# Weighted expert masks: from eight TensorE turns and two copies a batch to one small turn and a trip through DRAM; one weight split a unit later

## The reference, cut to what matters

```
router_logits = xf @ Wr.T
probs = softmax(router_logits)
topw, topi = top_k(probs, 2)
expert_w = sum(one_hot(topi, 8) * topw[..., None], axis=1)
for each expert e:
    g_lora = xf @ Ag_e.T @ Bg_e.T * 2
    u_lora = xf @ Au_e.T @ Bu_e.T * 2
    h = silu(gate_base + g_lora) * (up_base + u_lora)
    d_delta = h @ Ad_e.T @ Bd_e.T * 2
    acc = acc + d_delta * expert_w[:, e]
```

## Time and profile before

| | |
|---|---|
| median of 3 runs | 714.2 us (712.54 to 715.79) |
| profiled execution, its own time | 712.47 us |
| its span (first to last instruction) | 710.7 us |
| outside the span | 1.77 us |
| PE busy | 688.0 us, 97% |
| DVE busy | 517.6 us, 73% |
| ACT busy | 376.0 us, 53% |
| granted TensorE clock, mean | 0.996 |

### The profile page before, as it was taken

One profiled execution on the slowest core, in us unless ns is written; L12 is line 12 of the kernel. 1 busy time (PEld: TensorE's weight loads), 2 busy tenths in 40 slices (PEclk: granted clock), 3 DMA queues, 4 the chain that ended last, 5 costly groups with the idle time before them and its releaser, 6 DMA issues.

```text
span 710.7 us, 10703 instructions
## 1 busy us (share of the span) xinstructions
PE 688.0 (97%) x4090; PEld 585.9 (82%) x4090; DVE 517.6 (73%) x933; ACT 376.0 (53%) x777; POOL 130.9 (18%) x125
## 2 busy tenths in 40 slices
PE   7999999999999999999999999999999999999997
PEld 7778888878777788887888878887777888889886
DVE  7736667886965658556675656757769998998996
ACT  5896676855745425354254442446557355354541
POOL 7145434510000010000200001000032214203220
PEclk9999999999999999999999999999999999999999
DMA  5096353000000000000000000050000000000000
GB/s 192 13 309 213 106 136 98 0 1 1 1 1 0 1 1 1 0 1 1 1 1 0 1 1 1 0 237 2 1 0 1 1 1 30 1 30 1 2 30 30
DMA packets 21282, 25.78 MB, mean 36 GB/s; under 512 B 976, under 2 KB 19408, under 8 KB 20464
## 3 DMA queue, kind: packets, MB, share of 16 engines
q1 hardware_dynamic: 20576, 23.79, 10.2%
q10 hardware_dynamic: 656, 1.31, 0.5%
HBM read 22.94 MB, written 2.16 MB: 35 GB/s over the span
## 4 chain that ended last, share of the span: by engine, by line
PE 70%; DVE 18%; issue 5%; ACT 4%; POOL 2%; DMA 1%; DVEq 0%; POOLq 0%
PE bank L89 21%; PE bank L91 19%; PE bank L90 19%; DVE l_ring_lo L2472 2%; PE bank L490 2%; DVE l_ge L2453 2%; DVE l_h L2468 2%; DVE l_o L2476 1%; DVE l_h L2425 1%; DVE h_raw L1186 1%; POOL m_den L827 1%; PE bank L466 1%; DVE fused_lo L141 1%; DVE l_oT_lo L2482 1%; POOL l_prod L2336 1%
## 5 line engine op out<-in xcount | busy, mean ns | idle before, releaser
L1186 DVE TENSOR_TENSOR h_raw<-h_s,bank 128x512 f32<-128x512 f32 x104 | 71.4, 687 | 113.8 <-ACT h_s L1176 98.8
L1176 ACT ACTIVATE h_s<-bank 128x512 f32<-128x512 f32 x104 | 62.2, 598 | 161.2 <-PE bank L91 161.1
L1191 DVE TENSOR_TENSOR h_ring_lo<-h_raw,h_ring_hi 128x512 fp32r<-128x512 f32 x92 | 69.0, 750 | 0.1
L1180 ACT ACTIVATE h_ring_hi<-h_raw 128x512 fp32r<-128x512 f32 x104 | 64.8, 623 | 2.3 <-DVE h_raw L1186 2.3
L90 PE MATMUL bank<-fused_lo,h_ring_hi 128*128 128x256 f32 x208 | 58.4, 281 | 0.0
L2173 ACT ACTIVATE l_s<-bank 128x512 f32<-128x512 f32 x32 | 19.1, 598 | 64.6 <-PE bank L91 64.6
L89 PE MATMUL bank<-l_xT_hi,l_wgu 128*128 128x512 f32 x128 | 51.3, 401 | 0.1
L89 PE MATMUL bank<-f_yT_hi,mlp_hi 128*128 128x512 f32 x128 | 50.9, 398 | 0.0
L90 PE MATMUL bank<-l_xT_lo,l_wgu 128*128 128x512 f32 x128 | 50.3, 393 | 0.0
L91 PE MATMUL bank<-l_xT_hi,l_lo 128*128 128x512 f32 x128 | 50.3, 393 | 0.0
L91 PE MATMUL bank<-f_yT_hi,fused_lo 128*128 128x512 f32 x128 | 50.0, 391 | 0.0
(11 more groups left out here) (363 smaller groups left out, 2022.8 us busy)
## 6 DMA issues: line engine op xcount, KB each, us to landing
m_W<-m_scratch SPq DMA_DIRECT2D x16, 512.0 KB, 6.2
fused_raw<-in_fused SPq DMA_DIRECT2D x1, 3584.0 KB, 16.0
res<-in_x SPq DMA_DIRECT2D x4, 512.0 KB, 6.1
fused_raw<-in_fused SPq DMA_DIRECT2D x2, 1024.0 KB, 8.3
l_raw<-in_layer SPq DMA_DIRECT2D x1, 2048.0 KB, 10.0
out_x<-res SPq DMA_DIRECT2D x16, 128.0 KB, 1.8
l_raw<-in_layer SPq DMA_DIRECT2D x1, 1280.0 KB, 12.5
fused_raw<-in_fused SPq DMA_DIRECT2D x1, 1152.0 KB, 5.1
```

Of the source, the lines that this page charges most:

```text
L1176: self.nc.scalar.activation(self.s[u % 2][r, :], gate[r, :], ACT.Silu).then_inc(self.silu.sem, 1)
L1180: self.nc.scalar.activation(self.unit(i, u)[0], self.product(i, u), ACT.Copy).then_inc(self.hi.sem, 1)
L1186: self.nc.vector.tensor_tensor(out=self.product(i, u), in0=self.s[u % 2][r, :], in1=up[r, :], op=ALU.mult).then_inc(self.hidden.sem, 1)
L1191: self.nc.vector.tensor_tensor(out=lo, in0=self.product(i, u), in1=f32(hi), op=ALU.subtract).then_inc(self.lo.sem, 1)
```

## The change

Four things are changed.

1. The weighted masks are no longer widened by DVE and turned by PE in eight 128x128 transposes. DVE writes both weighted tiles, [128, 32] each, side by side with the columns in the order (expert, chunk), and PE turns the 64 columns in one instruction (`turn_weights`, position 9). ACT copies the result, 64 rows x 128 tokens, to SBUF (`turned_sel`, in memory that `selx[2]` had).
2. SP stores these 64 rows to a DRAM tensor `expert_weights` (32 KB) and then loads each of the two [8, 512] halves back with every row repeated 16 times, into `mask[:, n, :]`: two DMAs of 256 KB.
3. The waits follow: `weigh_experts` waits for the two loads (`weights_spread`); `scale_y` of the next batch, whose output lies over `turned_sel`, waits for the store; the squeeze waits for the copy (t = 1) and for `operands(1)` (t = 2).
4. In the first batch the piece `squeeze` is split at position 10, not 9, by ACT and by DVE.

```diff
+        g.expert_weights = nc.dram_tensor("expert_weights", (B, 2, E, S), fp32, kind="Internal").ap()
...
-    SPLIT = {..., 8: ("down",), 9: ("squeeze",), 11: ("base2",), 12: ("back",)}
+    SPLIT = {..., 8: ("down",), 10: ("squeeze",), 11: ("base2",), 12: ("back",)}
...
+    turned_sel = selx[0:2 * C * E, 2, 0:P]
...
     @block.sync
-        sp.wait_ge(hid.down.sem, hid.down.at(B - 1, NF))
-        for n in range(len(l1.fetch.groups)):
-            l1.fetch.issue(sp, n)
+        for i in range(B):
+            if i == B - 1:
+                sp.wait_ge(hid.down.sem, hid.down.at(B - 1, NF))
+                for n in range(len(l1.fetch.groups)):
+                    l1.fetch.issue(sp, n)
+            sp.wait_ge(weights_in.sem, weights_in.at(i, 1))
+            sp.dma_start(g.expert_weights[i].rearrange("n e (c s) -> (n e c) s", s=P), turned_sel).then_inc(weights_stored.sem, 16)
+            sp.wait_ge(weights_stored.sem, weights_stored.at(i, 16))
+            for n in range(2):
+                sp.dma_start(mask[:, n, :], g.expert_weights[i, n].unsqueeze(1).to_broadcast([E, RK, S])).then_inc(weights_spread.sem, 16)
...
     # PE, down(i, u), first slice of a choice t
-                    pe.wait_ge(mask_in.sem, mask_in.at(i, t))
+                    if t == 1:
+                        pe.wait_ge(weights_in.sem, weights_in.at(i, 1))
+                    else:
+                        pe.wait_ge(ops[1].sem, ops[1].at(i, 4))
...
-            elif n >= 2:
-                pe.wait_ge(ops[n - 2].sem, ops[n - 2].at(i, 4))
-                    last = nc.tensor.transpose(turn_bank[n % 2][:, chunk(c)], selx[:, n, c * ER:(c + 1) * ER], ident[:, :])
...
+        def turn_weights(i):
+            pe.wait_ge(weights_ready.sem, weights_ready.at(i, 2))
+            pe.wait_ge(ops[0].sem, ops[0].at(i, 4))
+            nc.tensor.transpose(turn_bank[0][0:2 * C * E, 0:P], sel[:, 2:4, :].rearrange("p n x -> p (n x)"), ident[:, :]).then_inc(weights_t.sem, 1)
...
                 elif u == 9:
-                    turn_mask(i, 2)
-                elif u == 10:
-                    turn_mask(i, 3)
+                    turn_weights(i)
...
-        def copy_mask(i, n):
-            act.wait_ge(mask_t.sem, mask_t.at(i, n + 3))
-            nc.scalar.activation(mask[:, n, :], turn_bank[n][:, :], ACT.Copy).then_inc(mask_in.sem, 1)
+        def copy_weights(i):
+            act.wait_ge(weights_t.sem, weights_t.at(i, 1))
+            nc.scalar.activation(turned_sel, turn_bank[0][0:2 * C * E, 0:P], ACT.Copy).then_inc(weights_in.sem, 1)
...
     # DVE
         def scale_y(i):
-            dve.wait_ge(mask_t.sem, mask_t.at(i - 1, 4))
+            dve.wait_ge(weights_stored.sem, weights_stored.at(i - 1, 16))
...
-            for n in (2, 3):
-                spread_out(n)
...
         def weigh_experts(i):
+            dve.wait_ge(weights_spread.sem, weights_spread.at(i, 32))
```

More of the change, by code:

```diff
@@ L1329, in fused_phase @@
     splitting, known = opening.splitting, opening.known
-    SPLIT = {0: ("mlp3",), 1: ("router", "ranks", "mlp4"), 2: ("mlp5",), 3: ("mlp_down4",), 4: ("mlp6",), 5: ("mlp7",), 6: ("base0",), 7: ("expand",), 8: ("down",), 9: ("squeeze",), 11: ("base2",), 12: ("back",)}
+    SPLIT = {0: ("mlp3",), 1: ("router", "ranks", "mlp4"), 2: ("mlp5",), 3: ("mlp_down4",), 4: ("mlp6",), 5: ("mlp7",), 6: ("base0",), 7: ("expand",), 8: ("down",), 10: ("squeeze",), 11: ("base2",), 12: ("back",)}
     SPLIT_NEXT = {15: (0, 2), 17: (2, 3), 19: (3, 4), 20: (4, 5), 21: (5, 6), 23: (6, 7)}
@@ L1371, in fused_phase @@
     a_done, a_hi, a_lo = sg("f_a", 2), sg("f_ahi", 2), sg("f_alo", 2)
-    spread, mask_t, mask_in, ops = sg("f_spread", 4), sg("f_maskt", 4), sg("f_maskin", 2), [sg("f_ops1", 4), sg("f_ops2", 4)]
+    weights_ready, weights_t, weights_in, weights_stored, weights_spread = (sg("f_weights" + n, k) for n, k in (("", 2), ("_t", 1), ("_in", 1), ("_stored", 16), ("_spread", 32)))
+    spread, mask_t, ops = sg("f_spread", 2), sg("f_maskt", 2), [sg("f_ops1", 4), sg("f_ops2", 4)]
     zprod, zsum, zhi, zlo, experts_done = sg("f_zprod", 2), sg("f_zsum", 1), sg("f_zhi", 1), sg("f_zlo", 1), sg("f_experts", 1)
     both, acc_free, late_ready, late_done = sg("f_both", 1), sg("f_accfree", 2), sg("f_late", 1), sg("f_late_done", 2)
-    NPRE, NLATE = 18, 11
+    NPRE, NLATE = 16, 11
     pre_sem, late_steps = g.sems("f_pre"), sg("f_late_steps", NLATE)
@@ L1511, in turn_mask @@
                 pe.wait_ge(a_lo.sem, a_lo.at(i, 2))
-            elif n >= 2:
-                pe.wait_ge(ops[n - 2].sem, ops[n - 2].at(i, 4))
             for c in range(C):
-                if n < 2:
-                    last = nc.tensor.matmul(turn_bank[n][:, chunk(c)], exact[n][:, c * ER:(c + 1) * ER], ident16, start=True, stop=True)
-                else:
-                    last = nc.tensor.transpose(turn_bank[n % 2][:, chunk(c)], selx[:, n, c * ER:(c + 1) * ER], ident[:, :])
+                last = nc.tensor.matmul(turn_bank[n][:, chunk(c)], exact[n][:, c * ER:(c + 1) * ER], ident16, start=True, stop=True)
             last.then_inc(mask_t.sem, 1)
+        def turn_weights(i):
+            pe.wait_ge(weights_ready.sem, weights_ready.at(i, 2))
+            pe.wait_ge(ops[0].sem, ops[0].at(i, 4))
+            nc.tensor.transpose(turn_bank[0][0:2 * C * E, 0:P], sel[:, 2:4, :].rearrange("p n x -> p (n x)"), ident[:, :]).then_inc(weights_t.sem, 1)
         def experts_back(i):
@@ L1630, in _ @@
                     exponentials(i)
-                elif u in (9, 10):
-                    copy_mask(i, u - 9)
+                elif u == 9:
+                    copy_weights(i)
                 elif u == TURN - 1 and i < B - 1:
@@ L1696, in norm_x @@
             if i:
[L1697 removed]
+                dve.wait_ge(mask_t.sem, mask_t.at(i - 1, 2))
             for c in (2 * half, 2 * half + 1):
@@ L1724, in spread_out @@
         def spread_out(n):
-            wide = exact[n] if n < 2 else selx[:, n, :]
-            nc.vector.tensor_copy(wide.rearrange("p (x r) -> p x r", r=RK), expand(sel[:, n, :], RK)).then_inc(spread.sem, 1)
+            nc.vector.tensor_copy(exact[n].rearrange("p (x r) -> p x r", r=RK), expand(sel[:, n, :], RK)).then_inc(spread.sem, 1)
         def first_expert(i, w):
@@ L1763, in weigh @@
             dve.wait_ge(w.sem, w.done())
-            nc.vector.tensor_tensor(out=sel[:, 2, :], in0=sel[:, 0, :], in1=small[2][:, :], op=ALU.mult).then_inc(w.sem, w.one())
-            nc.vector.scalar_tensor_tensor(out=sel[:, 3, :], in0=small[6][:, :], scalar=2.0, in1=small[2][:, :], op0=ALU.mult, op1=ALU.mult).then_inc(w.sem, w.one())
-            dve.wait_ge(w.sem, w.done())
-            for n in (2, 3):
-                spread_out(n)
+            by_expert = lambda n: sel[:, n, :].rearrange("p (e c) -> p c e", e=E)
+            nc.vector.tensor_tensor(out=by_expert(2), in0=sel[:, 0, :].rearrange("p (c e) -> p c e", e=E), in1=per_token(small[2]), op=ALU.mult).then_inc(weights_ready.sem, 1)
+            nc.vector.scalar_tensor_tensor(out=by_expert(3), in0=per_token(small[6]), scalar=2.0, in1=per_token(small[2]),
+                                           op0=ALU.mult, op1=ALU.mult).then_inc(weights_ready.sem, 1)
         def operands(i, t):
@@ L1863, in fused_phase @@
     rest.zprod, rest.zsum, rest.zhi, rest.zlo, rest.back, rest.back_added = zprod, zsum, zhi, zlo, experts_done, acc_free
-    rest.mask_t, rest.both, rest.hid = mask_t, both, hid
+    rest.weights_stored, rest.weights_spread, rest.both, rest.hid = weights_stored, weights_spread, both, hid
     rest.stats, rest.late_done, rest.stat_steps = late_ready, late_done, late_steps
@@ L2377, in weigh_experts @@
             x = token_cols(n)
+            dve.wait_ge(rest.weights_spread.sem, rest.weights_spread.at(B - 1, 32))
             for t in range(2):
```

## The result

The changed kernel takes 711.4 us (median of 20 runs, 708.99 to 713.32); the kernel before, run beside it 20 times, 714.85. The ratio is 0.9952, 95% interval 0.9941 to 0.9962: 3.4 us or 0.48% faster. The forecast was 3.7 us, 0.52%. The measured median is 0.9 us above the forecast one; 0.65 of that is the median of before, which over 20 runs was 714.85 and not the 714.2 that the forecast started from.

The account below looks back on a forecast made before the run. PE's stream was taken to bound the later batches, DVE's order the window from 188 to 200 us in the first. 2.3 + 1.35 = 3.7 us (1.9 to 4.5) took the median from 714.2 to 710.5 us; range 707.2 to 713.2.

Parts of the forecast that it names:

- PE slots: PE's stream in batches 1 to 3: a matmul costs its 0.11 us slot; three batches save 2.3 us (1.9 to 2.7).
- Rival B: PE's turns: a removed matmul is worth its whole duration, 7.6 us in all, giving 706.6 us; chance 0.10.
- the agreement that the prediction speaks of: PE's turns: the trace's 273 ns a matmul agrees with the skill page's about 275 ns for a transpose.
- Batches 1 to 3: PE's stream: two weighted turns removed, one matmul added, saving 0.78 us a batch (0.62 to 0.89).
- nothing on DVE or ACT matters unless it becomes late: Second batch, PE busy 90.84 of 91 us: each removed PE instruction shortens the batch by its slot.
- Batch 0: First batch, chain through DVE and ACT to down(11): saves 1.35 us, bounds nothing and 1.8.
- Had the split stayed in place: First batch at down(9): with the squeeze split unmoved PE would wait until 192.82, the removed turn worth nothing.
- The DMAs: Store and mask loads cost nothing: 16 and 45 us of cover in batch 0, 28 us in the last.
- C: Whole change: the gain is eaten by unseen waits, late weights or DMA writes into SBUF; 712.5 to 715 us; chance 0.12.
- D: Last batch: masks land late behind 4 MB in SP's queue, so the kernel is slower, about 718 us; chance 0.08.
- Rival A: First batch: ACT's base2 split does not follow gates(11), only 2.3 us remain, 711.9 us; chance 0.16.
- the 0.5% line: Whole kernel: a measurement can tell about 0.5%, 3.6 us, from no change; the forecast of 0.52% lies on it.

Follow-up runs that it names:

- experiment 3: Changed kernel with the small turn of the weights issued eight times in a row; 714.07 us, ratio 0.9987 to the kernel before.
- Experiment 4: Changed kernel with two of the four products of operands(1) moved behind lo(9) on DVE; 710.85 us, ratio 0.9952 to the kernel before.
- experiment 5: Changed kernel with SP waiting for down(19) before it issues the two mask loads; 711.45 us, ratio 0.9956 to the kernel before.
- all splits early: Changed kernel with two operands(1) products behind lo(9) and every split from mlp7 on one or two positions earlier; 710.52 us, ratio 0.9941 to the kernel before.
- all but base2: Changed kernel with two operands(1) products behind lo(9) and splits from mlp7 on earlier, except base2 and back; 710.78 us, ratio 0.9945 to the kernel before.

## Why the prediction was right, and where it was off

*PE slots.* Right in kind and in price: a removed turn is worth 0.11 us a matmul (experiment 3), the small turn costs 0.10, and nothing of the recorded 0.27 us counts beyond the slot. Rival B is out, and with it the reading of the Trainium skill's 275 ns ("TensorE: Matmul & The Clock Gate", Part 4: PE-mode transpose) as a cost. The page gives that figure for a 128x128 transpose in bf16. The trace has none of that form, so the agreement that the prediction speaks of is one between different forms: the float32 transposes here are recorded with 272 and 273 ns.

*Batches 1 to 3, forecast 0.78 us each, measured 0.60, 0.62 and 0.61.* The step that was off is "nothing on DVE or ACT matters unless it becomes late", and I did not ask what becomes late when PE is 0.8 us ahead: lo(9), by 0.17 us, because DVE makes four operands first. It was not late before, so no row of before showed a wait; it was to be found by setting lo(9)'s place in DVE's queue against `down(9)` less 0.8 us. Experiment 4 took that wait away and the batches gave 0.79, 0.81 and 0.76.

*Batch 0, forecast 1.35 us, measured 1.48.* The chain holds at each step, with times moved by 3.09 us: `down(8)` unchanged but for 0.08, which makes up most of the difference of 0.13, since everything behind it follows it; `down(9)` forecast at 192.0, seen at 191.93; ACT's base2 split forecast to end at 194.32, seen at 194.18; `down(11)` forecast at 197.64, seen at 197.49, with 0.41 us of wait left where I had said 0.5. That DVE would gain nothing from its two copies, since ACT holds the `expand` split, is confirmed by the 0.60 us of idle time there.

*"Had the split stayed in place ... the removed turn would have been worth nothing: the two edits belong together."* Wrong. I followed that case to `down(9)` and not on to `down(11)`. There the 0.93 us wait goes without the moved split too, since ACT's base2 split follows `gates(11)`, which the missing turn frees. The masks alone save 1.11 us in the first batch, the split alone nothing, both 1.48: the split needs the masks, the masks don't need the split.

*The DMAs.* Free, as forecast: their time by experiment 5, their traffic by experiments 3 and 4 (batches 1 to 3 lose nothing beside the slots, and with lo(9) in time they give the slots' full price). Rivals C and D are out. The store was forecast at 1.6 us and took 1.8 to 3.5, in the last batch behind layer 1's loads 12.5 us as in the earlier trace rows. That the masks land 5 to 10 us behind the store is not shown, since no row has their landing.

*Rival A* did not occur: the base2 chain followed, with 0.20 us of DVE idle time ahead of it where I had counted on 0.3.

In sum 1.48 + 0.60 + 0.62 + 0.61 = 3.31 against 1.35 + 2.3 = 3.7: batches 1 to 3 gave 0.5 us less than forecast, the first 0.13 more. The range and the place at the 0.5% line held.

## What to carry to other kernels

On an engine that is always busy, price a removed instruction by the distance of starts around it, not by its duration; then move the engine ahead by that gain and look at each thing that it waits for, also those that it did not wait for before, and follow a chain to its last wait before saying what an edit is worth. A recorded wait can be shorter than the real one by the overlap of two matmuls (0.17 us here), and a wait shorter than that shows in no row at all. Work widened by copies (here sixteen times) may be cheaper narrow on PE and widened by a DMA, if its use is tens of microseconds away. Where runs of one kernel fall into groups some us apart, compare intervals between fixed points of the profiles, which repeated here to a few hundredths of a microsecond.

## What the runs showed of the hardware

The runs fall into groups: before, 6 of 20 at 712.5 to 712.7 us, 4 at 713.9 to 714.3, 8 at 715.4 to 715.8 and 2 at 716.6; after, 4 at 709.0 to 709.6, 6 at 710.5 to 710.7, 6 at 712.2 and 4 at 713.0 to 713.3. The groups lie in the same order with the mean granted clock of TensorE, 0.999, 0.995 to 0.997, 0.995 and 0.990 after the change, and each group moved by about 3.5 us. The profiles show where such a step arises: in the opening. Windows of 10 us of the kernel before:

```profile
10.00:20.00 10.00, 8.47 (x51) 7.72 (x52) 9.42 (x32) 9.21 (x18) 8.21 (x12) 0.83 0.19 76
...
30.00:40.00 10.00, 9.50 (x61) 7.92 (x62) 4.34 (x9) 7.96 (x19) 1.46 (x2) 1.00 0.44 115
```

and of the changed kernel, whose fused phase began 3.1 us later:

```profile
30.00:40.00 10.00, 9.46 (x56) 8.57 (x57) 3.83 (x8) 6.73 (x16) 0.99 (x1) 0.83 0.44 119
40.00:50.00 10.00, 8.65 (x48) 6.03 (x46) 3.81 (x5) 8.80 (x27) 5.52 (x7) 0.83 1.04 316
```

The granted clock is 0.83 over a window in which it stood for a third of the time at 1.2 instead of 2.4 GHz. In before's profile that fell once, between 10 and 20 us; in the changed kernel's it fell twice, between 30 and 50 us. Of the ten profiles of this study three begin the fused phase (PE's turn of `f_xs`) at about 150.0 us, five at 151.5 to 151.7 and two at 153.1 to 153.2, whichever kernel it is: steps of some 1.5 us. The same windows of all ten sort them in the same way: no such fall between 30 and 50 us in the first three (before, eight turns, all splits early), one in the five, two in the last two (changed, all but base2). A fall between 10 and 20 us stands in six of them and moves nothing: of the five with one later fall three have it and two don't. PE was busy for 8.5 to 9.5 of the 10 us in these windows; what decides when the clock falls was not tried.

The recorded duration of a float32 turn is the same for both widths that the traces show: 272 ns with 64 stationary columns, 273 with 128 (medians). The load of the stationary operand is not: 109 ns against 141.
